# Four transformer layers on one core: the spread of q and k cut into four pieces, one per head group, and steps of three layers placed elsewhere

## The reference

```python
xn = _layernorm(x, axis=-1)
x = x + _L0_attn_ref(xn, ...) + _L0_ffn_ref(xn, ...)   # the same again for L1, L2, L3
```

```python
energy = jnp.einsum('bhqd,bhkd->bhqk', q, k) + bias[None]
att = jax.nn.softmax(energy / (scaling * temp), axis=-1)
out = jnp.einsum('bhqk,bhkd->bhqd', att, v)
```

```python
S = g4 * S + jnp.einsum('bhi,bhj->bhij', kt, vt)
num = jnp.einsum('bhij,bhi->bhj', S, qt); den = jnp.sum(z * qt, axis=-1, keepdims=True) + EPS
y = (outputs * gate).reshape(b, t, H * DK);  return y @ W_O.T
```

## Time and profile before

| | us |
|---|---|
| median of 3 runs | 2657.45 |
| lowest and highest | 2647.17, 2663.92 |
| profiled execution, its own time | 2658.72 |
| span of that execution | 2656.90 |

### The profile page before, as it was taken

How to read it: one execution, slowest core, us unless ns; L and a number is a source line. 1 busy time by engine, 2 the same in 40 slices (tenths; PEclk the granted TensorE clock), 3 DMA queues, 4 the chain that set the end, 5 groups by cost and what they waited for, 6 DMA issues and landing times. The chain is left out here.

```text
span 2656.9 us, 45118 instructions
## 1 busy us (share of the span) xinstructions
PE 2307.9 (87%) x15319; PEld 1430.4 (54%) x15442; DVE 1556.5 (59%) x4327; ACT 1332.5 (50%) x2458; POOL 566.8 (21%) x591
## 2 busy tenths in 40 slices
PE   4898888999985798898977898988898989889986
PEld 2555554799982576677972444444453443344433
DVE  4777777111113677775334766666567777777762
ACT  3555555554544344341342545555554666666665
POOL 2333443000006566650011111111001100011100
PEclk9999999999996899999995989999998999999998
DMA  4222222577771001002651111111121101111101
GB/s 147 70 85 83 71 84 86 172 228 225 230 205 56 26 25 30 28 14 80 192 146 53 53 54 54 54 54 54 55 80 57 35 28 50 55 55 53 39 25 33
DMA packets 132516, 214.11 MB, mean 81 GB/s; under 512 B 22680, under 2 KB 91968, under 8 KB 125376
## 3 DMA queue, kind: packets, MB, share of 16 engines
q1 hardware_dynamic: 120080, 188.79, 23.6%
q0 software_dynamic: 10240, 20.99, 2.5%
q10 hardware_dynamic: 1968, 1.44, 0.2%
HBM read 158.57 MB, written 51.40 MB: 79 GB/s over the span
## 5 line engine op out<-in xcount | busy, mean ns | idle before, releaser
L558 DVE TENSOR_REDUCE arena<-bank 128x1 f32<-128x512 f32 (+4 forms) x1216 | 723.7, 615 | 406.6 <-PE bank L547 248.7
L633 ACT ACTIVATE arena<-bank 128x512 f32<-128x512 f32 x640 | 374.3, 599 | 385.7 <-PE bank L623 380.9
L541 PE MATMUL bank<-arena 125*128 125x512 bf16 (+3 forms) x1536 | 471.6, 345 | 26.7 <-DVE arena L558 11.0
L633 ACT ACTIVATE arena<-bank,inverse_scale 128x512 f32<-128x512 f32 x512 | 336.7, 688 | 197.1 <-PE bank L611 73.0
L611 PE MATMUL bank<-arena 128*128 128x512 bf16 (+3 forms) x1413 | 404.9, 331 | 29.1 <-DMA arena<-arena 17.6
L611 PEld LDWEIGHTS bank<-arena 128*128 128x128 bf16 x1536 | 140.1, 100 | 352.8 <-ACT arena L633 191.9
L648 PE MATMUL bank<-arena 128*32 128x512 f32 (+3 forms) x3072 | 325.6, 508 | 0.9 <-ACT arena L633 0.8
L962 POOL DMA_INDIRECT back_rows<-sorted_out,back_now x160 | 155.9, 974 | 496.6 <-PE bank L623 232.1
L541 PEld LDWEIGHTS bank<-arena 125*128 125x128 bf16 x1536 | 146.1, 101 | 197.1 <-DVE arena L558 86.2
L623 PE MATMUL bank<-mask_k,identb 128*128 128x256 bf16 (+1 forms) x640 | 165.1, 258 | 48.1 <-DMA arena<-arena 45.6
L1243 ACT ACTIVATE arena<-bank,arena 128x256 f32<-128x256 f32 x320 | 131.8, 470 | 144.6 <-PE bank L1293 144.6
(11 more groups left out here) (264 smaller groups left out, 3631.0 us busy)
## 6 DMA issues: line engine op xcount, KB each, us to landing
arena<-k_parts SPq DMA_DIRECT2D x48, 576.0 KB
arena<-q_parts SPq DMA_DIRECT2D x48, 576.0 KB
arena<-in_L_ffn_w SPq DMA_DIRECT2D x80, 320.0 KB, 3.6
arena<-in_L_ffn_w SPq DMA_DIRECT2D x80, 258.0 KB, 2.9
arena<-sorted_in SPq DMA_DIRECT2D x104, 128.0 KB, 2.8
sorted_out<-arena SPq DMA_DIRECT2D x104, 128.0 KB, 3.5
arena<-in_L_ffn_w SPq DMA_DIRECT2D x24, 512.0 KB, 3.8
k_parts<-arena SPq DMA_DIRECT2D x24, 384.0 KB
```

Of the source, the lines that this page charges most:

```text
L541: ins = pe.matmul(mx[:, k * w:(k + 1) * w], Qx[0:KMAX, h, q * P:(q + 1) * P], Kx[0:KMAX, h, 0:w], start=(k == 0 or not L.causal), stop=not ...
L558: ins = dve.reduce_max(L.mx[:, g % 2, q, heads[0]:heads[-1] + 1], mx[:, 0:w * len(heads) - far].rearrange("p (j k) -> p j k", k=w - far), ...
L633: act.activation(L.probs[:, n % L.PR, 0:w], st[:, 0:w], ACT.Exp, scale=L.scale).then_inc(L.st_free.sem, 1)
```

## The change

It has five parts.

1. The halves become four pieces (PIECES = NG), one per head group. A piece is again one DMA for Kx and one for Qx, now of 288 KB in rows of 4 KB, and both count on one semaphore, `L.spread[g]`. pe_max waits for its group's piece at every group's first step. In layers 0 and 2, `behind_row` is {2: 3, 3: 4}: pieces 0 and 1 are issued at once, piece 2 after three rows, piece 3 after four. In layer 3 it is {0: 2, 2: 3, 3: 4}. In a first batch each piece waits for the one before.
2. In layer 3 the steps max_rows, copy_rows and send_rows of group 1 are 0.8 slots later (`rows_late`).
3. In layer 0, batch 0 waits only for the padding of copy 0; the wait for copy 1's is at the same place of batch 1.
4. In layer 1, the sums of phi of batches 0 and 1 are made by VectorE. The state steps are 2.0 us later, divide and the odd weighted steps 0.7 to 1.6 us earlier, the last two turn_y 1.3 us earlier, the output product 1.4 us later.
5. In layer 2's batch 0, the rebuild steps from the third on (before: from the fifth on) lie among the maxima, from slot -17 at 2.0 slots each; loss and choose move from -8.2 and -7.4 to -4.5 and -3.7.

The diff's core:

```diff
-HALVES = 2
+PIECES = NG
...
-            L.behind_row = {0: 2} if biased else {1: 3}
+            L.rows_late = 0.8 if biased else 0.0
+            L.behind_row = {0: 2, 2: 3, 3: 4} if biased else {2: 3, 3: 4}
...
-            for half in range(HALVES):
-                heads = slice(half * H // HALVES, (half + 1) * H // HALVES)
-                if not first and half in L.behind_row:
+            for n, full in enumerate(L.spread):
+                heads = slice(n * HG, (n + 1) * HG)
+                if not first and n in L.behind_row:
                     settle(sp)
-                    sp.wait_ge(L.nmrow.sem, L.nmrow.at(whole(b.index - 1), 16 * L.behind_row[half]))
-                if first and half > 0:
-                    for one in (L.kx[0], L.qx[0]):
-                        settle(sp)
-                        sp.wait_ge(one.sem, one.at(b, 16))
+                    sp.wait_ge(L.nmrow.sem, L.nmrow.at(whole(b.index - 1), 16 * L.behind_row[n]))
+                if first and n > 0:
+                    settle(sp)
+                    sp.wait_ge(L.spread[n - 1].sem, L.spread[n - 1].at(b, 32))
...
-            if g % (NG // HALVES) == 0 and i == 0:
-                half = g * HALVES // NG
-                pe.wait_ge(L.kx[half].sem, L.kx[half].at(b, 16))
-                pe.wait_ge(L.qx[half].sem, L.qx[half].at(b, 16))
+            if i == 0:
+                pe.wait_ge(L.spread[g].sem, L.spread[g].at(b, 32))
...
-        def pe_attention_ready(pe, L):
+        def pe_attention_ready(pe, L, filled=None):
             pe.wait_ge(L.setup.sem, L.setup.at(2 * L.copies))
-            pe.wait_ge(L.padded.sem, L.padded.at(2 * L.copies))
+            pe.wait_ge(L.padded.sem, L.padded.at(2 * (filled or L.copies)))
...
-                    steps += [(begin - LAST_MAX + 3.2, "max_rows", g, 0, b),
-                              (begin - LAST_MAX + 3.8, "copy_rows", g, 0, b),
-                              (begin - LAST_MAX + 4.1, "send_rows", g, 0, b),
+                    turn = begin - LAST_MAX + (L.rows_late if g == 1 else 0.0)
+                    steps += [(turn + 3.2, "max_rows", g, 0, b),
+                              (turn + 3.8, "copy_rows", g, 0, b),
+                              (turn + 4.1, "send_rows", g, 0, b),
...
-                start = [(-41.5, "loaded", 0), (-35.0, "keys", 0), (-20.0, "filled", 0)] if n == 0 else []
+                start = [(-41.5, "loaded", 0), (-35.0, "keys", 0)] if n == 0 else []
+                start += [(-20.0, "filled", n + 1)] if n < L.copies else []
...
-                    steps += [(12.0 * m, "decayed", m), (12.0 * m + 5.0, "fade", m), (3.0 * m - 0.4, "state", m)]
-                    steps += [(weigh + 2.0, "weighted", 2 * m), (weigh + 4.9, "divide", 2 * m),
-                              (weigh + 5.6, "weighted", 2 * m + 1), (weigh + 8.2, "divide", 2 * m + 1)]
-                steps += [(at, "turn_y", c) for c, at in enumerate((34.5, 46.5, UNIT + 8.9, UNIT + 9.9))]
+                    steps += [(12.0 * m, "decayed", m), (12.0 * m + 5.0, "fade", m), (3.0 * m + 1.6, "state", m)]
+                    steps += [(weigh + 2.0, "weighted", 2 * m), (weigh + 4.2, "divide", 2 * m),
+                              (weigh + 4.6, "weighted", 2 * m + 1), (weigh + 6.6, "divide", 2 * m + 1)]
+                steps += [(at, "turn_y", c) for c, at in enumerate((34.5, 46.5, UNIT + 7.6, UNIT + 8.6))]
...
-                steps.append((UNIT + 12.2, "out", 0))
+                steps.append((UNIT + 13.6, "out", 0))
...
+                def phi(b, n):
+                    if b.index < 2:
+                        dve.wait_ge(L.exp_ready.sem, L.exp_ready.at(b, n + 1))
+                        dve.tensor_tensor(L.kq[b.parity]["kq"[n // FT]][:, n % FT, :], L.relu[:, n % 2, :],
+                                          L.neg[:, n % 2, :], ALU.add).then_inc(L.phi.sem, 1)
...
-                    step for e in range(E2) for at in [-17.0 + 2.2 * (e - 4) if n == 0 and e > 3 else -31.0 + 1.6 * e]
+                    step for e in range(E2) for at in [-17.0 + 2.0 * (e - 2) if n == 0 and e > 1 else -31.0 + 1.6 * e]
...
-                    (-8.2 if n == 0 else -15.2, "loss", 0), (-7.4 if n == 0 else -14.4, "choose", 0),
+                    (-4.5 if n == 0 else -15.2, "loss", 0), (-3.7 if n == 0 else -14.4, "choose", 0),
```

More of the change, by code:

```diff
@@ L294, in attention_plan @@
             L.stored = s("parts_stored", 16 * (1 + NPART), 1)
-            L.kx = [s(f"k_expanded{i}_", 16, 1) for i in range(HALVES)]
-            L.qx = [s(f"q_expanded{i}_", 16, 1) for i in range(HALVES)]
+            L.spread = [s(f"heads_spread{i}_", 32, 1) for i in range(PIECES)]
             L.nmrow = s("max_rows_in", 16 * NG, 1)
@@ L304, in attention_plan @@
             L.po_free = s("attended_free", NG, 1)
-            L.started += [L.qsplit, L.stored, *L.kx, *L.qx, L.nmrow, L.st_full]
+            L.started += [L.qsplit, L.stored, *L.spread, L.nmrow, L.st_full]
             L.init = [L.mx_free, L.st_free, L.p_free, L.po_free]
@@ L487, in sp_expand @@
         def sp_expand(sp, L, b, first=False):
-            for one in L.kx + L.qx:
+            for one in L.spread:
                 sp.wait_ge(one.sem, one.at(b, 0))
@@ L1228, in gate, with filled @@
                     act.activation(L.ev[:], L.ev[:], ACT.Exp).then_inc(L.gate_exp.sem, 1)
-                def filled(act, L, b, _):
-                    act_attention_setup(act, L, 1)
+                def filled(act, L, b, copies):
+                    if b.index == 0:
+                        act_attention_setup(act, L, 1)
                 L.own_act = {"loaded": loaded, "filled": filled, "gate_exp": gate}
@@ L1255, in keys, with filled @@
                     pe.wait_ge(L.keys_squared, 3)
-                def filled(pe, L, b, _):
-                    pe_attention_ready(pe, L)
+                def filled(pe, L, b, copies):
+                    pe_attention_ready(pe, L, copies)
                 def logit(pe, L, b, _):
@@ L1507, in layer1 @@
             UNIT = 12.0 * H1 // 2
-            LATER = {"dve": {"decayed": 0.8, "turn_y": 0.8, "out": 1.0, "logit": 0.8, "rank": 1.0, "turn_k": 0.8, "state": 0.8},
+            LATER = {"dve": {"decayed": 0.8, "turn_y": 0.8, "out": 1.0, "logit": 0.8, "rank": 1.0, "turn_k": 0.8, "state": 0.8, "phi": 1.6},
                      "act": {"norm": 0.7, "phi": 0.7, "gate": 0.7, "value": 0.7},
@@ L1590, in phi @@
                 def phi(b, n):
+                    if b.index < 2:
+                        return
                     dst = L.kq[b.parity]["kq"[n // FT]][:, n % FT, :]
@@ L1593, in phi @@
                     if n == 0:
+                        pool.wait_ge(L.phi.sem, L.phi.at(b, 0))
                         for name in (f"s{h}" for h in (H1 - 2, H1 - 1)):
@@ L1963, in add_rows @@
                     dve_add_pair(dve, L.before, b, p)
-                each_trip(dve, {"decay": decay, "locate": locate, "table": table, "add_rows": add_rows, "center": center, "scale": scale, "logit": logit, "rank": rank, "turn_k": turn_k,
+                each_trip(dve, {"decay": decay, "locate": locate, "table": table, "add_rows": add_rows, "center": center, "scale": scale, "phi": phi, "logit": logit, "rank": rank, "turn_k": turn_k,
                                 "state": state, "fade": fade, "decayed": decayed, "divide": divide,
```

4 lines of the change are left out of this document (2 added, 2 removed).

## The result

The changed kernel took 2589.32 us (median of 4 runs, 2585.11 to 2590.63) beside 2655.16 for the one before (now over four runs): a ratio of 0.9749, with a 95% interval of 0.9715 to 0.9782. Measured a second time, with the experiments, it took 2578.04 us (2568.99 to 2589.31) beside 2652.12: 0.9718 (0.9669 to 0.9768). It is faster by 2.2 to 3.3%, inside the range; the gain is 66 to 74 us where I had said 89. The spans of the two profiled executions are 2588.8 and 2570.4 us, against 2656.9.

A forecast was written before the change was run, and what follows sets the result against it. TensorE was taken to set the pace everywhere, standing still 5.5 to 8.7 us a batch. Terms 47.5 + 7 + 7 + 20 + 3.4 + 4 = 88.9 off 2658.7 gave 2569.8, said as 2570 us; range 2546 to 2614.

The forecast's parts named there:

- A: Four pieces in layers 0, 2 and 3: rows of maxima land before TensorE wants them; 47.5 us, bounds 26 to 52.7.
- B: Layer 3's group 1 transposes (L590), placed 0.8 slots later, wait less for VectorE: 7 of 10.7 us, 0 to 10.7.
- E: Layer 2's first batch: moved rebuild, loss and choice steps fill TensorE's gaps while VectorE reduces; 3.4 us, 0 to 6.
- F: Granted clock, low after some stalls: with 20 stalls gone, 4 us gained, 0 to 10.
- My margin of 1.6 us: Layer 3: the row lands near 2051.5, TensorE wants it at 2053.13, so its wait goes with 1.6 us in hand.
- C: Layer 0's start: the 5.10 us padding wait moves to batch 1, a later row's wait shrinks; 7 us, 2 to 7.3.
- D: Layer 1: moved steps and VectorE's phi adds mostly fill three TensorE waits; 20 of 25 us, 5 to 25.
- the packet sets the price: Rival: packets cost the same whatever they hold, a piece takes 11 us, layer 0's rows come late; near 2780; chance 0.03.
- Half the gain in the softmax layers: Rival: the row still meets a piece's tail, or VectorE takes the pace; 47.5 becomes 24, hence 2593; chance 0.17.
- The small risk that I had named at SyncE: Layer 2's last batch: loads of layer 3's bias table start some 10 us later behind the new wait; 0 to 3 us.

The follow-up runs named there:

- the pieces alone: The kernel before with only the halves cut into four pieces, no later step in layer 3 and no other part: 2598.10 us, ratio 0.9793.
- the last kernel: Changed kernel with layer 3's pieces behind later rows, layer 2's differ earlier, its pieces later save in its last batch, Q part in three DMAs: 2531.24 us.

## Why the prediction was right, and what was mis-sized

It was right in sign and range, and in the mechanism of layers 0 and 2; 2570 was 19 us under the first measurement and 8 under the second. Of the 88.9 us the first pair of profiles shows 68.1. The 20.8 that are missing are 9.4 in layer 3 (22.8 for A and B, 13.4 came), 6.1 in layer 2 (15.8 for A and E, 9.7 came), 3.8 in layer 1 and F's 4; layer 0 gave 2.9 more than forecast, and the rest is -0.4. The second profile of the changed kernel shows 86.5. Term by term, against the first profile of the changed kernel:

**A in layers 0 and 2, right.** I gave them 90% of 21.4 and 13.8, 19 and 12 us. Layer 0's batches gained 21.7, since the falls of the clock that had followed its waits went too (17 us at the lower level before, none after), which is term F. In the changed kernel piece 2 and the row pass one another as I had worked out: the piece is issued at 135.83, the row at 142.26, and piece 3 at 144.68, when the row has landed; no wait for it shows.

```profile
135.83 0.80 SPq L515 DMA_DIRECT2D arena<-k_parts  x1
...
142.26 0.76 ACTq L523 DMA_DIRECT2D arena<-arena  x1
...
144.68 0.77 SPq L515 DMA_DIRECT2D arena<-k_parts  x1
```

Layer 2's waits of the earlier trace rows went, 16.0 to 0 (1.8 in the second profile). Its gain was 11.4 us in one profile and 23.2 in the other, for the reason below.

**A in layer 3, mis-sized.** This step failed: I read the distance between the spread and the row from the earlier trace rows, which is the first boundary, and took it for all seven. There the first DMA is issued 12.55 us ahead of the row. At a steady boundary SyncE has the loads of the two experts and the stores of parts ahead of the spread, which is issued only 8.4 us ahead of the row. Before, and after:

```profile
2119.22 0.80 SPq L516 DMA_DIRECT2D arena<-k_parts  x1
...
2127.65 0.73 ACTq L524 DMA_DIRECT2D arena<-arena  x1
...
2134.02 0.39 PE L611 MATMUL bank<-arena 128*128 128x512 bf16 x1 [2.49 <-DMA arena<-arena]
```

```profile
2063.07 0.80 SPq L515 DMA_DIRECT2D arena<-k_parts  x1
...
2069.71 0.73 ACTq L523 DMA_DIRECT2D arena<-arena  x1
...
2075.38 0.39 PE L608 MATMUL bank<-arena 128*128 128x512 bf16 x1 [1.79 <-DMA arena<-arena]
```

So pieces 0 and 1, though half as long, were still under way when the row was sent, 6.6 us into a transfer of 13: it landed 1.8 us late, where it had been 2.5 late. My picture that the row "comes out behind" the transfer was wrong too. Before, its last packet was through at 2133.2, and the spread ran on to 2143.9. The row is held up 3 to 4 us beside either length of transfer, so a shorter one helps little until it is over before the row is sent. L608's waits went from 17.6 to 10.5 and not to under 3. I had 15.8 for this and 7 for B; both together brought 13.4. The run with the pieces behind the third row shows that nothing else stood there: the waits went to 0. My margin of 1.6 us was right as arithmetic and held for one boundary of seven (the first, where the row is sent 12.3 us behind the first DMA, has no wait in the changed kernel). No row shows the 1.5 us of start-up in that sum; the first packet of the spread came 1.6 us after the start of its issue, where my 0.8 + 1.5 make 2.3. And the slices of the earlier trace rows fall to 82 GB/s after some 3 us, not after 2.

**B, about right:** 7 forecast, 3 to 6 measured.

**C, right sum and wrong reason.** The start of layer 0 gained 7.5 us where I had 7; but 7.1 of it come with the pieces alone. The 5.1 us of the padding wait, which I booked in full, are worth 0.4 between these two profiles (3.2 with the changed kernel's second profile), and the row of the first group became the next to wait for. I had written that a stall removed may be taken by TensorE's next wait and gave it only to the low bound. The fixed cost of 2.0 us that I cited from the Trainium skill ("DMA: Bandwidth & Descriptors", Anatomy of one DMA) is given there for DMAs issued from GpSimd; in this chain on SyncE's queue 1.9 us lie between the last packet of a piece and the first of the next.

**D, right sum, mostly another mechanism:** 20 forecast, 16.2 and 22.4 in the two profiles. I had it from waits of every batch, filled by a later place. The wait for the state fell (12.4 with VectorE's part, to 5.3) and that for GpSimd's sums went. But 10 of the 16 us, and 16 of the 22, lie ahead of the first output product, where VectorE's sums replaced GpSimd's; a steady batch mostly went from 48.1 to 47.6 us. The sums and the moved steps ran only together, so that the sums did it is not shown. The pieces alone, without this part, already have the state's wait at 4.8 and layer 1 at 422.0. And the output product's wait is 11.4 us in four of the twelve profiles with the part and 3.0 to 4.6 in others, at steady batches of 47.4 to 48.0 us either way (but for one of 49.7): that wait set no pace.

**E, nothing** where I had 3.4. TensorE's idle time in the lead-in and first batch is cut otherwise and not less.

**F** was the term that I understood least. I took 4 us with 0 to 10, as if the falls followed the row's waits alone. In layer 2 they follow another wait. In the nine profiles of changed kernels that have the wait of 1.57 us for the differ there are 54 steady batches; in 34 a fall begins within 2.3 us of that wait, and lasts 3.4 to 13.7 us (with the kernel before, 40 of 60). The four kernels without it have 8 falls in 24 batches, and the last of them none. Five of the eight stand behind a row's wait of 0.95 to 2.24 us, one behind 1.04 us for VectorE. The other two come among the same rebuild products with no wait over 0.5 us in the 10 us ahead, so the kind of work may still have a part. Which of the batches it strikes differs from one execution to the next of the same program (six of six, then two of six). Why is open: it was not tried apart from the waits. F's 4 us did not come in layer 2 in the first profile (51 us at the lower level for 55), and did in the second (14 us).

**The rivals.** That the packet sets the price fell as the rows had it: 288 packets of 8 KB took 22.7 to 23.1 us and 288 of 4 KB took 11.4 to 12.1. Half the gain in the softmax layers held for layer 3 only. The small risk that I had named at SyncE, the table's loads, did not strike in the changed kernel and did strike, with 5.7 us, in the kernel that moved layer 2's pieces further.

## What to carry to other kernels

A transfer whose outermost dimension is 3 ran at 76 to 82 GB/s for most of its time, and a small urgent one with the same shape, sent meanwhile, took 4.8 to 5.9 us instead of 1.6. Cut it so that it is over in time (layers 0 and 2), start it when the small one has landed, or give it a larger outermost dimension (layer 3); each took the wait away in steady batches here. Read the distance between two events at a steady boundary, and at two of them, before multiplying it. A wait of TensorE of 1.6 us can cost twice its length again by the clock that follows (an estimate: 10.2 us at 0.31 are 3.2). A kernel with such waits seems to scatter more: four runs of one lay 5.5 to 24 us apart, and 5.5 to 9 without them.

## What the runs showed of the hardware

The granted clock fell to its lower level at single waits of 1.57 us on an otherwise busy TensorE, in 34 of 54 cases. The batch of layer 2 that took 69.8 us in the changed kernel, 13.7 of them at the lower level, took 62.8 at full clock throughout in the last kernel, which also lacks the 1.57 us. A DMA of 12 KB took 1.6 us alone, 4.8 to 5.9 beside the spread in layer 3 and 2.4 to 3.2 beside the spread with its Q part in three. And a piece spread over more engines did not get faster in proportion: its 4 KB packets took 0.265 us each on average instead of 0.194.
